# One accumulator bank, later row maxima and a first image's layer in halves: a two-layer attention kernel with routed experts

## The reference, cut to what matters

```
# 1. convolutional attention, 4 heads of 32 channels, per image
q, k, v = split(qkv_weight @ group_norm(x))
attn = softmax(q^T k / sqrt(128))          # 1024 x 1024 for each head
x = x + out_weight @ (attn v) + out_bias
# 2. linear attention over tokens t (1024 x 128), 8 heads of 16
n = layer_norm(t)
keys = Wk n + bk; K = softmax of keys over all positions
Q = softmax of (Wq n + bq) over the 16 channels of a head; V = Wv n + bv
t = t + Wr (K V^T Q) + br
# 3. experts: each token goes to the 2 best of 8
n = layer_norm(t); weights, expert = top2(softmax(n @ router_w + router_b))
t = t + sum over the two of weight * (gelu(layer_norm(n)*ln_g+ln_b @ W1 + b1) @ W2 + b2)
```

## Time and profile before

| what | value |
|---|---|
| median of 3 runs | 363.25 us |
| span of the profiled execution, first to last instruction | 384.2 us |
| granted TensorE clock, mean | 0.929 |
| TensorE matmul busy | 334.2 us (87%) |
| VectorE, ACT, POOL busy | 202.1, 204.4, 110.8 us |
| first and last exponential of the attention stage | 44.8 and 209.7 us |

### The profile page before, as it was taken

The page is one execution under the profiler, slowest core; times in us unless marked ns, Lnnn a source line. Parts: engine busy times, 40 slices in busy tenths (PEclk is TensorE's granted clock), DMA queues, the critical chain, the costliest instruction groups (busy, mean ns, idle before and its releaser), DMA issues.

```text
span 384.2 us, 6582 instructions
## 1 busy us (share of the span) xinstructions
PE 334.2 (87%) x2004; PEld 211.5 (55%) x2004; DVE 202.1 (53%) x616; ACT 204.4 (53%) x324; POOL 110.8 (29%) x140
## 2 busy tenths in 40 slices
PE   7879799899999989999998496967551999999996
PEld 3533343333333335445432354867551999999996
DVE  2584444563756553565576248666402455777620
ACT  1460765666576554655585023665212677777732
POOL 2082291000000001000307630061774344444430
PEclk9985989999999999999999879996665899999999
DMA  6078768660000025000001102010211222222415
GB/s 186 2 149 194 170 146 333 154 243 34 0 2 3 3 72 149 0 2 1 2 0 43 55 8 62 16 28 23 62 62 34 64 72 70 71 66 79 143 37 210
DMA packets 21772, 29.28 MB, mean 76 GB/s; under 512 B 4055, under 2 KB 15628, under 8 KB 21484
## 3 DMA queue, kind: packets, MB, share of 16 engines
q1 hardware_dynamic: 16808, 18.04, 17.7%
q0 software_dynamic: 3744, 10.31, 8.4%
q10 hardware_dynamic: 1188, 0.53, 0.6%
HBM read 11.62 MB, written 9.25 MB: 54 GB/s over the span
## 4 chain that ended last, share of the span: by engine, by line
PE 70%; DVE 13%; issue 6%; another core or an unknown queue 4%; ACT 3%; DMA 1%; POOL 1%; DVEq 0%; SPq 0%; ACTq 0%; POOLq 0%
PE ps L864 15%; PE ps L1081 10%; PE ps L1068 9%; PE ps L845 6%; PE ps L826 6%; DVE above L1189 4%; PE ps L706 2%; PE ps L806 2%; PE ps L922 2%; PE ps L746 2%; PE ps L899 2%; PE ps L778 1%; PE ps L891 1%; DMA Qs<-mrow 1%
## 5 line engine op out<-in xcount | busy, mean ns | idle before, releaser
L558 ACT ACTIVATE probs<-ps 128x1024 f32<-128x1024 f32 x64 | 65.3, 1021 | 37.0 <-PE ps L845 36.9
L1081 PE MATMUL ps<-w,GT 128*128 x368 | 55.0, 297 | 18.8 <-ACT GT L684 15.0
L864 PE MATMUL ps<-probs,vT 128*32 128x512 f32 x256 | 68.2, 608 | 1.1 <-ACT probs L558 1.1
L864 PE MATMUL ps<-probs,ones 128*32 128x512 f32 x256 | 68.2, 609 | 0.0
L1081 PEld LDWEIGHTS ps<-w,GT 128*128 128x128 f32 x368 | 49.3, 208 | 22.0 <-issue 21.7
L1189 DVE CUSTOM_DVE_ANT_0 above<-ps,above 128x512 f32<-128x512 f32 x56 | 38.7, 691 | 40.8 <-PE ps L826 39.0
L496 POOL DMA_INDIRECT token_out<-Y,yidx x46 | 44.2, 961 | 48.2 <-DVE Y L1480 46.6
L433 POOL TENSOR_TENSOR rstd<-ve,minus_half 128x1 f32<-128x1 f32 (+2 forms) x6 | 10.3, 1724 | 160.6 <-DVE ve L1231 88.6
L1068 PE MATMUL ps<-XTT,w1s 128*128 128x128 f32 x368 | 53.1, 291 | 3.2 <-issue 3.2
L684 ACT ACTIVATE GT<-H 128x512 f32<-128x512 f32 x46 | 28.9, 629 | 46.5 <-DVE H L1469 27.4
L1068 PEld LDWEIGHTS ps<-XTT,w1s 128*128 128x128 f32 x368 | 49.2, 208 | 4.3 <-issue 4.3
(11 more groups left out here) (196 smaller groups left out, 427.5 us busy)
## 6 DMA issues: line engine op xcount, KB each, us to landing
expert_in<-zeros POOLq DMA_DIRECT2D x2, 1495.0 KB, 7.6
XR<-expert_in SPq DMA_DIRECT2D x46, 65.0 KB
Qs<-q_hi SPq DMA_DIRECT2D x16, 128.0 KB, 3.1
w<-in_L_ffn_W SPq DMA_DIRECT2D x1, 2048.0 KB, 8.4
w<-in_L_ffn_W SPq DMA_DIRECT2D x8, 256.0 KB, 4.1
YG<-token_out SPq DMA_DIRECT2D x8, 256.0 KB, 4.1
Ks<-k_hi SPq DMA_DIRECT2D x14, 128.0 KB, 2.6
X<-in_x SPq DMA_DIRECT2D x2, 512.0 KB, 4.6
```

What stands on the lines that cost most here:

```text
L558: nc.scalar.activation(probs[:, s % 3, :], bank(2 + 2 * (s % 2), 2), ACT.Exp).then_inc(exp_done, 1)
L864: last = nc.tensor.matmul(bank(6 + o % 2)[i * HD:(i + 1) * HD, :], w, probs[:, s % 3, hd * HALF:(hd + 1) * HALF], start=kt == 0, stop=kt = ...
L1081: last = nc.tensor.matmul(bank(4 + p)[:, 0:D], GT[:, p, c, :], w2[:, e, c, :], start=c == 0, stop=c == HC - 1)
```

## The change

1. All halves accumulate in bank 6 (ACC). When half o is complete, at the step s with s % 8 == 0, ACT copies the bank to `acc` in SBUF (`acc_copy`), behind the exponential of s; the next half waits for the copy, and VectorE closes from `acc`. Only the last half is closed from the bank.
2. Bank 7 (SPARE) is then free for image 0's layer 1 while slots still use 0 and 1. Its parts go through this one bank: tokens, keys and the transposed keys in two halves, queries and values in four quarters, each half or quarter waiting until the one before is copied or added out of the bank. The key exponential reads SBUF. From the queries' transpose on all is as before, one step later (48 to 58 for 47 to 57).
3. Slots: two in each of the steps 0 to 7, then 46 over the steps 8 to 45. The last is in step 45.
4. POOL writes the zero rows when the second row of maxima has landed, not the first.

The diff, cut to its core:

```diff
+        acc = sb("acc", [P, HALF])
+        ACC, SPARE = 6, 7
-        QV_BANK = ((0, 0), (2, 4))
+        QV_BANK = (2, 4)
...
+        BRISK, MAXIMA_END = 8, 46
+
         def slots_by(s):
-            return min(SLOTS, AHEAD + -(-(SLOTS - AHEAD) * s // (2 * STEPS)))
+            brisk = AHEAD + 2 * min(s, BRISK)
+            return min(SLOTS, brisk + -(-(SLOTS - AHEAD - 2 * BRISK) * max(0, s - BRISK) // (MAXIMA_END - BRISK)))
...
-        LAYER1_AT = {BEGIN_LAYER1: "centre residual", 34: "project", 35: "tokens_stats tokens", 38: "keys",
-                     40: "keys_exp", 41: "query_value0", 42: "query_value1", 43: "keyT query_max",
-                     44: "keyT_sb queries_exp", 45: "queries context", 46: "queries_scaled fold", 47: "queryT",
...
+        LAYER1_AT = {BEGIN_LAYER1: "centre", 34: "tokens_in0", 35: "tokens_in1 tokens_stats", 37: "tokens",
+                     38: "keys0", 39: "keys1", 40: "keys_exp query_value0", 41: "query_value1", 42: "query_value2",
+                     43: "query_value3", 44: "keyT0 query_max", 45: "keyT1 queries_exp", 46: "queries context",
+                     47: "queries_scaled fold", 48: "queryT", 49: "queryT_sb", 50: "attend stats", 51: "tokenT",
+                     52: "tokenT_sb", 53: "logits shift", 54: "gates_exp", 55: "route choose norm2_0", 56: "norm2_1",
+                     57: "norm2_2 counts", 58: "norm2_3"}
...
-            pool.wait_ge(mrow_in[0], 16 * 2)
+            pool.wait_ge(mrow_in[1], 16 * 2)
...
+            def acc_copy(o):
+                act.wait_ge(pv_done, KT * (o + 1))
+                if o:
+                    act.wait_ge(o_used, o)
+                nc.scalar.activation(acc[:, :], bank(ACC), ACT.Copy).then_inc(acc_copied, 1)
...
+            def a_key_copy(h):
+                act.wait_ge(keys_ready, h + 1)
+                nc.scalar.activation(EK[:, h * HALF:(h + 1) * HALF], bank(SPARE), ACT.Copy).then_inc(key_copied, 1)
...
                 exps(s // STEPS, s % STEPS)
+                if s % KT == 0 and s:
+                    acc_copy(s // KT - 1)
                 if s:
                     for g in new_slots(s - 1)[1:]:
                         max_above(g)
...
-                        if o >= 2:
-                            pe.wait_ge(o_used, o - 1)
+                        if o:
+                            pe.wait_ge(acc_copied, o)
...
-                    last = nc.tensor.matmul(bank(6 + o % 2)[i * HD:(i + 1) * HD, :], w,
+                    last = nc.tensor.matmul(bank(ACC)[i * HD:(i + 1) * HD, :], w,
...
+            def tokens_half(b, h):
+                o = bank(2 + h if b else SPARE)
+                pe.wait_ge(resid_ready, b + 1)
+                if b:
+                    pe.wait_ge(exp_done, UNITS * STEPS - 1)
+                elif h == 0:
+                    pe.wait_ge(rw_centred, 1)
+                else:
+                    pe.wait_ge(t_sb, 1)
+                for i in range(J // 2):
+                    nc.tensor.matmul(o[:, i * P:(i + 1) * P], XP[:, b, 4 * h + i, :], ident[:, :], start=i == 0, stop=False)
...
+            def t_keys_half(h):
+                pe.wait_ge(F_ready, h + 1)
+                if h:
+                    pe.wait_ge(key_half, h)
+                    pe.wait_ge(key_copied, h)
+                nc.tensor.matmul(bank(SPARE), wT[:, 6, :], F[:, 4 * h:4 * h + 4, :].rearrange("d j c -> d (j c)"),
+                                 start=True, stop=True).then_inc(keys_ready, 1)
+
+            def t_query_value_quarter(c):
+                if c == 0:
+                    pe.wait_ge(key_half, 2)
+                    pe.wait_ge(key_copied, 2)
+                else:
+                    pe.wait_ge(qv_sb, c)
...
             def norm_sums(o):
-                dve.wait_ge(pv_done, (o + 1) * KT)
+                if o < 2 * UNITS - 1:
+                    dve.wait_ge(acc_copied, o + 1)
+                else:
+                    dve.wait_ge(pv_done, (o + 1) * KT)
...
+            def v_key_half(h):
+                dve.wait_ge(keys_ready, h + 1)
+                nc.vector.tensor_reduce(kneg[:, 2 + h:3 + h], bank(SPARE), AX, ALU.max, negate=True).then_inc(key_half, 1)
```

More of the change, by code:

```diff
@@ L909, in t_keys @@
                 last.then_inc(keys_ready, 1)
[L911 to L916, removed]
-                else:
[L918 to L921, removed]
-                    last = nc.tensor.matmul(bank(QV_BANK[b][h], 2)[:, i * 2 * P:(i + 1) * 2 * P], F[:, 4 * h + i, :],
+            def t_keys_half(h):
[5 more added lines that the diff above has]
+                                 start=True, stop=True).then_inc(keys_ready, 1)
@@ L923, in t_query_value @@
+            def t_query_value_quarter(c):
+                if c == 0:
+                    pe.wait_ge(key_half, 2)
+                    pe.wait_ge(key_copied, 2)
+                else:
+                    pe.wait_ge(qv_sb, c)
+                for i in range(2):
+                    last = nc.tensor.matmul(bank(SPARE)[:, i * 2 * P:(i + 1) * 2 * P], F[:, 2 * c + i, :],
                                             wT[:, 4:6, :].rearrange("d w k -> d (w k)"), start=True, stop=True)
                 last.then_inc(qv_ready, 1)
+            def t_query_value(b, h):
+                if h == 0:
+                    t_filler()
+                pe.wait_ge(F_ready, 2 * b + h + 1)
+                for i in range(J // 2):
+                    last = nc.tensor.matmul(bank(QV_BANK[h], 2)[:, i * 2 * P:(i + 1) * 2 * P], F[:, 4 * h + i, :],
+                                            wT[:, 4:6, :].rearrange("d w k -> d (w k)"), start=True, stop=True)
+                last.then_inc(qv_ready, 1)
@@ L926, in t_keyT, with t_keyT_half @@
+            def t_keyT_half(h):
+                pe.wait_ge(ek_ready, 1)
+                if h == 0:
+                    pe.wait_ge(qv_sb, QV_DONE[0])
+                else:
+                    pe.wait_ge(ekT_sb, h)
+                for i in range(J // 2):
+                    j = 4 * h + i
+                    last = nc.tensor.transpose(bank(SPARE)[:, i * P:(i + 1) * P], EK[:, j * P:(j + 1) * P], ident[:, :])
+                last.then_inc(ekT_ready, 1)
             def t_keyT(b):
                 pe.wait_ge(ek_ready, b + 1)
-                pe.wait_ge(qv_sb, 2 * b + 2)
+                pe.wait_ge(qv_sb, QV_DONE[b])
@@ L1200, in max_slot, with closed @@
                                                    ALU.mult, ALU.subtract).then_inc(mhl_ready, 1)
+            def closed(o):
+                return acc if o < 2 * UNITS - 1 else bank(ACC)
             def norm_sums(o):
-                dve.wait_ge(pv_done, (o + 1) * KT)
+                if o < 2 * UNITS - 1:
+                    dve.wait_ge(acc_copied, o + 1)
+                else:
+                    dve.wait_ge(pv_done, (o + 1) * KT)
                 if o:
                     dve.wait_ge(o_used, o)
-                link(nc.vector.transpose(sums[:, :], bank(6 + o % 2)[64:128, :]))
+                link(nc.vector.transpose(sums[:, :], closed(o)[64:128, :]))
             def norm_reciprocal():
@@ L1216, in norm_product @@
                 place = attn[64 * pair:64 * pair + 64, b, :].rearrange("c (j p) -> c p j", j=J)[:, qh * 64:(qh + 1) * 64, :]
[L1217 removed]
+                nc.vector.tensor_tensor(place, closed(o)[0:64, :].rearrange("c (p j) -> c p j", j=J),
                                         rec[:, :].rearrange("c (p j) -> c p j", j=J), ALU.mult).then_inc(o_used, 1)
@@ L1246, in v_centre @@
                     dve.wait_ge(means_ready, 1)
-                    nc.vector.scalar_tensor_tensor(rw[:, :], ps[:, 0:E], -1.0 / D, rw[:, :], ALU.mult,
+                    nc.vector.scalar_tensor_tensor(rw[:, :], bank(SPARE)[:, 0:E], -1.0 / D, rw[:, :], ALU.mult,
                                                    ALU.add).then_inc(rw_centred, 1)
```

108 lines of the change are left out of this document (68 added, 40 removed).

## The result

The changed kernel takes 372.33 us (median of 4 runs, 372.01 to 373.17); the kernel before, on the same chip, 363.28 (4 runs). The ratio is 1.0254, with a 95% interval of 1.0234 to 1.0275: 9.05 us slower, where 8.05 were forecast. The profiled execution took 372.01 us and its span is 370.2, so this trace is in line with the timed runs.

A forecast was written before the change was run, and what follows sets the result against it. TensorE was taken to bound the attention stage: 11.15 us of waits added less 4.3 removed is 6.8, with one later step of 1.66 8.4. On 363.25 that gives 371.6, with half the product's gain 371.3 (range 366.5 to 374.5).

The forecast's parts named there:

- as worked out: Main case: attention stage 6.8 us later, scatter 8.4 later, all of it passing through POOL; chance 0.50.
- Unexplained waits of the profiled execution left out of the sum: VectorE's 11.1, 6.5 and 4.3 us behind the attention stage, taken as delays of the profiled execution only.
- POOL is the later one, by 1.3: Before image 1's norm, POOL's 14 scatters end 1.3 us after the power's input; rival, POOL not later: chance 0.22.
- The added waits: New TensorE waits from slots sharing steps with layer 1 and copies ahead of relus: 11.15 us in sum.
- the centring: Step 33: TensorE waits for VectorE's closing work and centring, 1.6 us.
- the third quarter: Steps 41 and 42: third query/value quarter waits for the second to leave the bank, 2.5 us, the largest.
- step 8's relu: Step 8: accumulator copy stands ahead of slot 25's relu on ACT; TensorE waits 1.0 us.
- Removed waits: 4.3 us: step 8's row load 1.3, heavy steps' row maxima 1.4, last row transpose 0.7, residual 0.9.
- The product from SBUF: Product's operand now in SBUF: price between 0.8 and 1.05, changing the sum by 0.5; half that gain taken.
- The step that failed: Attention stage: each slot costs TensorE 0.64 us wherever it stands, so spreading 62 slots over 46 steps buys none.
- none by more: Sign of being right: steps up to 31 shorter by 0.64 us for each slot gone, none by more.
- The rival with a chance of 0.08, the falling clock: TensorE's clock falls in stretches with waits: one fall costs 2 to 3 us, two give 376; chance 0.08.

The follow-up runs named there:

- Experiment 1: Kernel before with only the zero rows moved behind the second row of maxima: 362.38 us, ratio 0.9986.
- experiment 4: Changed kernel with POOL's power for image 1's norm behind the 12th scatter instead of the 14th: 368.41 us, ratio 1.0133.
- experiment 8: Kernel before with zero rows late and POOL's power for image 1's norm one pair of scatters earlier: 359.05 us, ratio 0.9885.
- experiment 12: Kernel before with POOL's power one pair of scatters earlier alone, zero rows where they were: 360.71 us, ratio 0.9915.
- experiment 3: Changed kernel with ACT's relu of a step's slot ahead of its layer copies, key maximum behind the key copy: 367.64 us, ratio 1.0129.
- experiment 11: Changed kernel with four queue orders turned (relu, accumulator copy, layer part, POOL's power), the key maximum's wait and one more filler matmul: 355.20 us, ratio 0.9752.
- experiment 5: Changed kernel with 10 instead of 6 unread filler matmuls ahead of image 1's queries and values: 369.97 us, ratio 1.0174.
- after: The changed kernel itself, as in its profiled execution, against the kernel before: 372.33 us, ratio 1.0254.
- experiment 6: Changed kernel with the accumulator's copy behind the step's relu copies in ACT's queue: 371.28 us, ratio 1.0211.
- experiment 9: Changed kernel with the zero rows early again, behind the first row of maxima: 376.08 us, ratio 1.0342.

## Why the prediction was right, and where it wasn't

**The answer** (slower, 371.3, 366.5 to 374.5) was right: 372.33. Its case "as worked out" held for the order of events; its terms did not all, and that the number came so near is partly luck (below).

- *Unexplained waits of the profiled execution left out of the sum*: right. Experiment 1's trace has none; its execution took 364.0 beside a median of 362.38.
- *POOL is the later one, by 1.3*: right, shown by experiments 1, 4, 8 and 12. The power stood behind its input by 1.9 in experiment 1's trace and by 3.6 after the change, where 2.9 were forecast.
- *The added waits*: of those that the trace can tell apart, the centring 1.7 (1.6), the third quarter 2.1 (2.5), step 8's relu 1.04 (1.0), step 32's row maximum 1.15 (1.1), the last row transpose 0.86 (0.8) came as written. At step 36 TensorE waits 1.03 for the row maximum behind the statistics (1.4). ACT's order was worth 4.7 us in all (experiment 3), more than its terms at 34, 35, 38 and 39 to 46 (1.05 + 1.1 + 0.8 + 0.4 = 3.35); 0.7 of the difference is the clock in the two traces.
- *Removed waits*: the row's load did land in time, 1.0 for 1.3 forecast, and alone it is worth 0.9 us by the medians (experiment 1). It was in 2.3 us after its issue, within the 3.7 that the prediction asked for. The 2.0 us that the prediction takes from the Trainium skill ("DMA: Bandwidth & Descriptors", Anatomy of one DMA) are given there for DMAs that POOL issues, and SP issues this one; its 2.3 are in keeping with them. The relu at step 8 takes the 1.0 back, so that the steps 4 to 9 are as long as before (15.57 for 15.54), as the sum had it.
- *The product from SBUF* was to give back half of 0.5 us. It takes 1.03 us from `acc` and 1.04 from PSUM: that gain isn't there.
- **The step that failed** is the one put in bold: "Spreading the 62 slots over 46 steps therefore buys no TensorE time: each slot costs 0.64 wherever it stands." A step without slots takes 1.66, with one 2.13, with two 2.95. The first slot costs 0.47, the second 0.82. The chain of a one-slot step, after the change, is TensorE alone:

```profile
89.92 1.00 PE ps L900 x8
90.92 0.43 PE ps L842
91.35 0.47 PE ps L881 x2
91.81 0.24 PE ps L862
92.05 0.99 PE ps L900 x8
```

  Two scores take 0.47, a matmul's turn is some 0.24, and the 0.32 was the mean of five that the earlier trace rows holds, a first one (0.43) and a piece of 0.48 among them. The two-slot step of the earlier trace rows is a loop over VectorE's row maximum of 0.69; the prediction quoted that row and read the step as TensorE's. So the spread did buy something: 12.75 us for 17 slots, 1.9 more than 17 x 0.64, where the prediction's sign of being right was 0.64 for each slot gone "none by more". Its sum had 1.4 of this as waits for row maxima in heavy steps. What it had nowhere is the other end: a slot that comes first in its step costs 0.47 there, not 0.64. For 17 slots that makes 2.9 us too much, an estimate from these steps that no run isolates. In experiment 11, with the other orders, the steps 4 to 60 take 141.4 against 146.5 with late zero rows alone.
- **The rival with a chance of 0.08, the falling clock, came about.** It was put aside because the longest wait in the stage was to be 2.5 us and a fall had been seen behind 5. One came behind a wait of 2.1 us and cost 1.7 (steps 41 and 42), and others behind the stage, where the filler recovered 2.4 us (experiment 5). The forecast was still near because errors of both signs met. The stage was forecast 6.8 us longer; it is 5.7 longer with the 1.7 of the clock, so its waits and slots came to 4.0. These 2.8 too many stood against 1.7 of clock in the stage and another 1.7 us behind it, neither of which the sum had. That is luck.
- The sum, as the traces have it: attention stage +5.7 (with the clock's 1.7 and the row load's -1.0 in it), the scatter's step +1.66, together 7.3 to the first scatter, where 8.4 were forecast. The other 1.7 of the 9.05 come behind it. The clock is what the traces show there (from power to power POOL takes 29.4 us in after and 26.9 in experiment 1), but not all of the filler's 2.4 can be new: the 16 matmuls took 5.4 in experiment 1's trace as well.

Left open: why the same wait lowers the clock in one execution of the schedule and not in another (experiments 3, 5, 6 and 9), and how often it does so in the timed executions, whose times alone don't tell.

## What to carry to other kernels

Price a wait of TensorE as a range: the wait alone (1.7 here) to the wait plus what runs at half clock behind it (3.2). Look for the second part in the length of the same instruction at two places. Before work is spread out to clear a queue, read the chain of a full and of a half-full step: what differs isn't the number of instructions but who closes the loop. And when a change that frees a resource comes out slower, turn the order in the other engines' queues before giving it up: nearly the same parts in another order went from 2.5% slower to 2.5% faster, of which 1.2% could be had without the change (experiment 8).

## What was not expected of the hardware

- Filler matmuls as a gain: 4 of them, 3.4 us of TensorE's time in a gap that was there anyway, made the run 2.4 us shorter.
- The granted clock fell after 2.1 us of standing still in one case (0.50 in 166 to 168) and stayed at 1.00 behind a wait of 1.7 in another (133 to 139, after), where in experiments 3, 5 and 9 the same wait brought 0.50. In experiments 3 and 5 the 2.1 us left it at 1.00.
- One profiled execution of the kernel before was 21 us longer than its timed runs, by waits for which no record has a cause; the thirteen others of this case had none of it. A profile is one execution, and its span should be laid beside the median before its rows are summed.
